# Moving the value matmuls to the end of each TensorE step in an attention and SwiGLU kernel

## The reference

```python
xn = _layernorm(x, axis=-1)
# attention: 16 heads of 8 columns, 4 key/value heads, rotary embedding
scores = jnp.einsum('bthd,bshd->btsh', q, k) * scale
probs = jax.nn.softmax(scores, axis=2)
context = jnp.einsum('btsh,bshd->bthd', probs, v).reshape(b, t, DIM)
attn = context @ Wo.T + bo
# SwiGLU, weights dequantised from int32
h = jax.nn.silu(gate) * up
ffn = jnp.einsum('bsh,dh->bsd', h, wd)
x = x + attn + ffn
```

## Time and profile before

| what | value |
|---|---|
| median of three runs | 862.16 us (860.84 to 863.3) |
| the profiled execution | 862.28 us |
| its span | 860.1 us |
| TensorE busy (matmul) | 788.5 us, 92% |
| TensorE weight loads busy | 250.0 us, 29% |
| VectorE busy | 736.2 us, 86% |
| ScalarE busy | 594.8 us, 69% |
| GpSimd busy | 111.3 us, 13% |
| granted TensorE clock, mean | 0.959 |

### The profile page before, as it was taken

The page is one execution under the profiler, slowest core; times in us unless marked ns, Lnnn a source line. Parts: engine busy times, 40 slices in busy tenths (PEclk is TensorE's granted clock), DMA queues, the critical chain, the costliest instruction groups (busy, mean ns, idle before and its releaser), DMA issues.

```text
span 860.1 us, 18056 instructions
## 1 busy us (share of the span) xinstructions
PE 788.5 (92%) x4856; PEld 250.0 (29%) x4856; DVE 736.2 (86%) x1363; ACT 594.8 (69%) x1171; POOL 111.3 (13%) x205
## 2 busy tenths in 40 slices
PE   3597999989999999989999999989999999999996
PEld 2221333223232223223232223223232223223352
DVE  7587999979998899969998899979998899999841
ACT  2432778767876778757876778767876778777854
POOL 4154423407000000000000000000000000000000
PEclk9695999999999999989999999999999899999998
DMA  6302121212100001011110001011110001010021
GB/s 198 91 1 62 42 58 31 64 31 65 29 28 21 26 14 32 25 30 28 29 28 21 24 15 31 26 30 28 29 28 24 19 18 31 26 29 1 2 62 37
DMA packets 29220, 30.35 MB, mean 35 GB/s; under 512 B 6672, under 2 KB 21264, under 8 KB 29008
## 3 DMA queue, kind: packets, MB, share of 16 engines
q1 hardware_dynamic: 27552, 25.05, 10.5%
q0 software_dynamic: 720, 2.36, 0.9%
q10 hardware_dynamic: 864, 2.15, 0.7%
HBM read 23.12 MB, written 6.03 MB: 34 GB/s over the span
## 4 chain that ended last, share of the span: by engine, by line
PE 71%; ACT 12%; issue 7%; DVE 4%; DMA 3%; SPq 2%; ACTq 1%; DVEq 0%
PE acc_ps L934 28%; PE banks L848 16%; PE banks L865 13%; ACT probs L532 9%; PE banks L940 5%; PE banks L949 3%; PE banks L957 2%; ACT acc_sb L590 2%; DMA qc<-neg_max_T 2%; PE banks L974 1%; DVE mx L686 1%; PE banks L818 1%; PE banks L824 1%; SPq L324 1%; PE banks L853 1%
## 5 line engine op out<-in xcount | busy, mean ns | idle before, releaser
L686 DVE TENSOR_REDUCE mx<-banks 128x1 f32<-128x512 f32 x1024 | 631.6, 683 | 55.6 <-PE banks L848 39.4
L532 ACT ACTIVATE probs<-banks 128x512 f32<-128x512 f32 x1024 | 537.4, 604 | 198.0 <-PE banks L865 180.4
L865 PE MATMUL banks<-qc,kc 51*128 51x512 bf16 x1024 | 321.8, 390 | 18.7 <-ACT probs L532 7.4
L848 PE MATMUL banks<-ka,qa 48*128 48x512 bf16 x1024 | 292.8, 392 | 20.2 <-DMA qa<-q_parts 8.1
L934 PE MATMUL acc_ps<-probs,v_grp 128*32 128x512 f32 x2048 | 278.5, 616 | 0.7 <-ACT probs L532 0.7
L848 PEld LDWEIGHTS banks<-ka,qa 48*128 48x128 bf16 x1024 | 77.6, 95 | 326.4 <-DVE mx L686 255.2
L865 PEld LDWEIGHTS banks<-qc,kc 51*128 51x128 bf16 x1024 | 78.0, 94 | 143.1 <-ACT probs L532 138.7
L418 POOL TENSOR_TENSOR neg_max<-row_max,nought 128x16 bf16<-128x16 f32 x31 | 6.9, 221 | 545.1 <-DVE row_max L692 545.1
L934 PEld LDWEIGHTS acc_ps<-probs,v_grp 128*32 128x32 f32 x2048 | 40.5, 108 | 57.3 <-issue 44.3
L940 PE MATMUL banks<-xn_T,w_ffn 128*128 (+1 forms) x192 | 56.1, 416 | 0.0
L732 DVE SCALAR_TENSOR_TENSOR gated<-th,banks 128x256 f32<-128x256 f32 x48 | 20.2, 421 | 21.9 <-ACT th L581 18.2
(11 more groups left out here) (90 smaller groups left out, 271.0 us busy)
## 6 DMA issues: line engine op xcount, KB each, us to landing
qa<-q_parts SPq DMA_DIRECT2D x32, 96.0 KB
qc<-q_parts SPq DMA_DIRECT2D x64, 48.0 KB
q_parts<-part POOLq DMA_DIRECT2D x9, 256.0 KB, 3.7
y_all<-in_x SPq DMA_DIRECT2D x4, 512.0 KB, 9.6
qa<-q_parts SPq DMA_DIRECT2D x32, 64.0 KB
qc<-q_parts SPq DMA_DIRECT2D x64, 32.0 KB
out<-y_all SPq DMA_DIRECT2D x8, 256.0 KB, 2.3
ka<-k_parts SPq DMA_DIRECT2D x32, 48.0 KB
```

Source lines behind the costliest of these rows:

```text
L532: nc.scalar.activation(probs[:, s % SLOTS, j, :], banks[:, score_bank(G * s + j), :], ACT.Exp, scale=SCALE).then_inc(exp_done, 1)
L686: nc.vector.tensor_reduce(out=mx[:, h, col, k:k + 1], in_=ps, op=ALU.max, axis=AX.X).then_inc(max_done, 1)
L848: nc.tensor.matmul(ps, qa[par][rows, j // 2, t * P:(t + 1) * P], ka[par][rows, k * W:(k + 1) * W], start=True, stop=True).then_inc(a_ready, 1)
L865: nc.tensor.matmul(banks[:, score_bank(u), :], kc[par][rows, kt * P:(kt + 1) * P], qc[par][rows, h, j // 2, :], start=True, stop=True).the ...
```

## The change

In TensorE's `group` function the call of `weigh` leaves the loop over the four turns and stands behind it. A step is now: m0 s0 m1 s1 m2 s2, job, m3 s3, W. In the steps of the last group without units it was s0 s1, job, s2, W, s3 and becomes s0 s1, job, s2 s3, W. No instruction is added or removed, no wait has another value, and the other engines' programs stay as they are. The prologue, which places the first `weigh` ahead of the last unit and score matmul, stays too.

```diff
--- before.py
+++ after.py
@@ -1052,13 +1052,12 @@
                             for _ in range(len(todo) - len(units)):
                                 take(g, par, slot, order)
                                 slot += 1
-                        if j == G - 1:
-                            weigh(g + s // STEPS, par if s < STEPS else 1 - par, s % STEPS)
                         if units:
                             take(g, par, slot, order)
                             slot += 1
                         if more:
                             next_scores(g, pair, par, s, j)
+                    weigh(g + s // STEPS, par if s < STEPS else 1 - par, s % STEPS)
                 for slot in range(slot, len(order)):
                     take(g, par, slot, order)
```

## The result

The changed kernel takes 839.91 us (median of four runs, 837.63 to 841.42). The kernel before took 862.73 us beside it (860.84 to 864.53). The ratio is 0.9733, with a 95% interval from 0.9701 to 0.9766: 2.7% faster. The prediction was 840.0. The total was right. Behind it CTX, DOWN, NEG_T and the steps 14 and 15 were sized wrongly, and their errors cancelled for the most part.

A forecast was written before the change was run, and what follows sets the result against it. Plain steps were balanced between a dependency loop and VectorE at 2.42 us, with jobs in series. Savings of 2.0 us per group, net 1.5, times fifteen groups: 862.3 - 22.5 = 839.8, taken as 840; forecast 832 to 848, all cases 828 to 859.

The forecast's parts named there:

- CTX: Steps with a CTX job, two per group: 3.24 us falls to 3.04, set by VectorE; 0.4 us saved per group.
- DOWN: The step with the DOWN job, one per group: 3.96 us falls to 3.53, set by TensorE; 0.43 us saved.
- NEG_T: Steps with a NEG_T job, two per group: 2.64 us falls to 2.42; 0.4 us saved per group.
- UP: Steps with an UP job, three per group: 3.49 us falls to 3.22, set by VectorE; 0.8 us saved per group.
- VectorE less: DOWN step: TensorE needs 3.53 us and VectorE less than that, so TensorE sets the step.
- hidden in the idle time: NEG_T steps: the job fits into TensorE's idle time, so 2.64 us becomes 2.42.
- W gets no new wait: Plain steps: W reads an exponential older than the one the fourth score matmul waits for, so moving it adds no wait.
- plain steps: 0: Steps without a job: the change gains nothing, they stay at 2.42 us, and VectorE's 2.42 would hide a gain.
- three signs of being wrong: Jobs start behind a wait on VectorE; plain steps grow above 2.42 us; a turn costs clearly more than 4.9 us.
- A part of the gain: Rival: VectorE frees the job's bank late by 0.48 us, UP and DOWN save nothing; 853 us (848 to 859.5), chance 0.17.
- It does nothing: Rival: the wait moves from the exponential to VectorE's bank in every kind of step; stays at 862 us, chance 0.08.
- Slower: Rival: at the loop's turn W stands exposed and the slow clock lasts longer, about 7 us per turn; 882 us, chance 0.12.

The follow-up runs named there:

- The runs on step 14: Changed kernel, loop written out, W of step 14 back ahead of m3 and s3: 802.3 us; with ScalarE's copy of the maxima one exponential earlier too: 797.49 us.

## Why the prediction was right, point by point

**The mechanism is right.** Jobs stood in series with the loop of W, first score matmul, exponential and fourth score matmul, and now they fill the half microsecond in it. UP, three times, saves 0.93 us per group (0.8 predicted). The prediction priced UP by VectorE, 3.22; two of the three are at 3.13 or 3.14, nearer to TensorE's own sum of 3.06, which lacked the 0.07 that the job waits for its bank.

**CTX was priced by the wrong engine.** The step took 2.75, which the prediction gives as TensorE's sum (its terms as printed, 1.4 + 0.31 + 1.00, make 2.71), and not VectorE's 3.04: -0.6 us per group. The prediction gave to one step all the work that VectorE gets in it. With four banks VectorE may be late by some reductions, and TensorE goes on.

**NEG_T and DOWN pay that debt.** They came to 2.94, 2.66 and 3.88 instead of 2.42, 2.42 and 3.53: +0.76 and +0.35 us per group. The step of the prediction that failed is "VectorE less" at DOWN and "hidden in the idle time" at NEG_T: both looked at VectorE's work inside the step, and not at what it still had to do from the UP or CTX before it. The runs with half reductions bear this out, since these steps shrink in them and CTX does not. The prediction did say that this back pressure exists and took the total down for it, from 2.0 to 1.5 us; that it was nearly the right amount is more luck than working, because the deduction was made of other things.

**Step 14 was overlooked.** "W gets no new wait" and "plain steps: 0" are false for the last score matmul of a group, which has its own rule for the bank. It cost 0.49, and 0.22 of it came back, since step 15 no longer shows the wait for the DMA that the prediction had left in place. The runs on step 14 show both: 7.2 us for the order, 4.8 for the DMA.

**The sum.** Against 45.77 the steps moved by UP -0.93, CTX -0.98, DOWN -0.08, NEG_T +0.33, step 14 +0.49, step 15 -0.22, plain +0.03: -1.36, where -1.5 was predicted. Fifteen groups give 20.4 and not 22.5. The last group was taken as 0, because nothing would move against its loop but the last W, and gave 3.1: its two UP steps with units fell by 0.34 and 0.35, which the prediction had not counted, six steps without units by 0.21 or 0.22 each, and from W of step 13 to the end it took 1.3 us less. That it filled the hole in the sum of the groups is luck.

**The prediction's own signs.** Two of its three signs of being wrong came up. Jobs do start behind a wait on VectorE: in 33 of 48 UP jobs and 29 of 32 CTX jobs the profile has the weight load wait for it, and in no such job of the kernel before. Step 14, a plain step, grew to 2.91. The total held all the same because the first wait is short (0.07 in UP, 0.34 in DOWN, nothing in CTX) and CTX gave more than it was credited with.

```profile
PEld banks L940 <- DVE mx L686: 15.2, 33, 0.8
...
PEld banks L957 <- DVE mx L686: 15.0, 29, 0.5
```

**The turn is neutral in the mean.** 5.2 and 5.1 us per turn in the traces, 5.4 and 5.1 by the runs without the loop. What a run pays there varies with the clock. At 1.2 GHz W takes 1.93 us, as here in the changed kernel:

```profile
275.39 1.93 PE L934 MATMUL acc_ps<-probs,v_grp 128*32 128x512 f32 x8
```

The window of that stretch shows the clock in the column before the last two (0.50, which is 1.2 GHz):

```profile
275.39:277.00 1.61, 1.61 (x9) 0.19 (x8) 1.61 (x3) 0.70 (x2) 0.00 (x0) 0.50 0.00 0
```

This followed all six turns in the trace of the kernel before and three of six in the changed one's. The prediction left the clock at nothing because idle time is moved and not made longer; the traces show a dearer turn with the slow clock and fewer of them, which cancel. The Trainium skill (TensorE: Matmul & The Clock Gate, "HAM oscillation — how this bites in real kernels") expects slow stretches behind idle gaps, and these traces agree behind nine of their twelve turns. The half microsecond of idle time in every plain step did not bring the clock down: the group at 408.87 has a granted clock of 1.00. Whether the new order makes slow stretches rarer, one trace of each can't say.

**The rivals.** "A part of the gain" was right in its mechanism: the job waits for the bank of m3. It costs 0.34 in DOWN and 0.07 in an UP step, and not the whole 0.48. "It does nothing" is out. "Slower" was right that a turn with the slow clock costs more, but by about 1 us and not 7, and only in three of six. The order that does run slower is one that the prediction did not think of, in which the job moves and W stays.

**Left open.** In straight-line code the changed kernel's plain steps take 2.48 or 2.49 us and not 2.42, while DOWN takes 3.68 and not 3.88, and a group is still 44.4; the kernel before keeps 2.42 there. Why the first score matmul waits longer for the DMA of the maxima in the groups that begin with a turn, though the turn is a dozen steps back, was not tried, nor was what VectorE and ScalarE do in the gap of the turn: only that it goes when the loop is written out. No trace of the kernel before has a turn without the slow clock, so the price of a turn at the high clock is known for the new order alone.

## What to carry to other kernels

Put a block that holds up a queue where the queue waits anyway; before counting the gain, write down for each moved instruction which buffer it needs, who frees that and what that engine still owes from the steps before. Look for the exceptions in a rotation of buffers (here one score matmul in 64), since a reordering exposes them, and a fixed wait such as a DMA may be hidden by the very loss that you remove. When an order works, see what it gets besides: by the traces, moving W also kept the job's bank early, the tanh in front of its queue and each unit beside a score matmul, and a second order that shared only the place of the job lost 39 us.

## What the runs showed of the hardware

A pass of the loop costs 5.1 to 5.4 us more than the same instructions in straight-line code: VectorE is idle 2.4 us and ScalarE 2.9 at its start, and the program without the loop is 30 to 32 us faster, more than the change itself. The time of the changed kernel also varies less without the loop (809.03 to 810.35, against 837.63 to 841.42); that of the kernel before does not (828.47 to 832.86, against 860.84 to 864.53).

Two bf16 matmuls of 48 and 51 rows that lie in different halves of the array's rows start together, and the pair costs 0.22 us, as one alone does. When the order puts two of the same half beside each other, they start 0.22 apart; a plain step with one such place took 2.61 us instead of 2.42.
